# Second layer, both ends: the wait ahead of ScalarE's first square roots is taken off, and the last block's expert steps are placed at other pairs

## The chip, the cores and the metric

The kernel runs on one core of one Trainium2 chip. The metric is the device time of one execution in microseconds (us); where several executions are compared, it is their median. The core has five engines with a program each: TensorE (PE, with its weight loads shown as PEld), VectorE (DVE), ScalarE (ACT), GpSimd (POOL) and SyncE (SP, which here only starts transfers). They meet at semaphores: one engine increments, another waits for a count.

## What is computed

Two transformer-like layers over 4 sequences of 512 tokens with 128 features. Only the second layer is touched. It is, cut to what matters:

```python
# attention of layer 1, for each sequence: X is (512, 128), q and k are (512, 64)
q, k = X @ Wq.T, X @ Wk.T
Vy = X @ Wy_w.T + Wy_b
e = relu(rho(q[:, None, :] + k[None, :, :]))      # rho: signed square root, eps 1e-8
scores = e @ Wphi                                 # (512, 512)
ex = exp(scores - max(scores))
out = (ex @ Vy + (sum_j ex * e) @ We_w.T + We_b * denom) / (denom + 1e-9)
# feed-forward of layer 1: all 8 experts for every token, weighted by the top-2 shares
z = (x @ w1[e] + b1[e]) * (x @ w2[e] + b2[e])
s = silu(z @ wg[e] + bg[e])
out = out + share[:, e] * (s @ w3[e] + b3[e])
x = x + attention + feed_forward
```

## The kernel before

`second_layer` does the attention's pairwise part and the experts at once. The rows of all four sequences are cut into MB = 32 blocks. A block m holds 32 "pairs", numbered by group gg (0 to 7, `GROUPS`) and column c (0 to 3, `QUADS`); a pair is a 128x512 tile of `feat`, which lies in the tensor that the profile calls arena. There are two halves of `feat`, j = 0 and 1, used in turn. Each block also carries one expert for one sequence.

For every pair of a block the kernel does this:

- a **feature**: relu(k + q), on VectorE (line 1037), ScalarE (line 1176) or GpSimd (lines 1305 and 1311);
- a **root**: ScalarE's square root over two groups, 8 pairs, at once (line 1188, 128x4096);
- a **score**: TensorE multiplies by phi and adds into `psS` (line 1328), 4 multiplies a group, which the trace shows as 8 records since fp32 goes through in two passes;
- after a block's last score the maximum and shift on VectorE (`largest`, lines 1043 and 1045), the exponentials on ScalarE (lines 1197 and 1200) and `split` on VectorE (line 1103), which makes `spread`;
- a **broadcast** on TensorE (line 1341), which lays one row of exponentials over all partitions in one of 3 PSUM banks, and a **product** with accumulation on VectorE (`reduce_pair`, line 1051) that uses it. The broadcast of pair k waits until product k - 3 is done, so TensorE runs at most three pairs ahead.

The order on each engine is written out by hand: inside each engine's `tile`, a table `work` says after which (gg, c) which other step is issued. The expert's steps of a block are: left and right product on TensorE (lines 1377 and 1385), z on VectorE (line 1077), `gate` on TensorE (line 1392, four multiplies named (f, half)), tanh on ScalarE (line 1225, which uses the halved gate bias `bgh`), `lift` (add one) on GpSimd (line 1287), `silu` on VectorE (line 1083), `down` on TensorE (line 1405, two halves of four multiplies), and `add_experts` on VectorE (line 1094, four steps of 128x128). The `down` and `add_experts` steps of block m stand in block m + 1.

At the **start** of the layer there is nothing yet to reduce. VectorE makes the features of two whole blocks (a loop of n = 0 to 15 with four features each). After n = 7 it copies the transposed shares (line 1143), halves the shares (line 1145) and halves the gate bias (line 1146, semaphore `bg_halved`). After n = 9 it runs `largest(0, 0)`, and after n = 10 it adds the b3 products (line 1153). ScalarE makes a root for each odd n: the first four belong to block 0. TensorE does scores 0 to 5 of block 0, then 16 small multiplies for b3 (line 1453), then scores 6 and 7.

At the **end**, after block 31's last product, GpSimd copies the accumulated sums (`place`, line 1279, two copies), TensorE runs `combine` (lines 1359 and 1363), and VectorE finishes (lines 1064 to 1069), adds the last expert's output (line 1094), and the result leaves by DMA. In this kernel block 31's `down` stands on TensorE after the last broadcast and ahead of `combine`.

ScalarE's program for the start, the only place in which `bg_halved` is waited for:

```python
act.wait_ge(bg_halved, 1)
for n in range(2 * GROUPS):
    if n % 2:
        roots(n // GROUPS, n // GROUPS, n % GROUPS, ahead=True)
    if n == GROUPS + AHEAD_EXP[1]:
        exponentials(0, 0, before=0)
        keep_left(0, 0, first=True)
```

Of the kernel before, what the change touches and what calls it, by code (L numbers as in the profile page):

```python
# [922 lines left out]
def second_layer(nc, g, sb):  # L923
# [24 lines left out]
    with ExitStack() as ctx:  # L948
# [81 lines left out]
        with nc.Block() as block:  # L1030
            @block.vector
            def _(dve):
# [73 lines left out]
                def tile(t, first=False, last=False):  # L1106
                    for j in range(2):
# [8 lines left out]
                            (4, 0): lambda: none or add_experts(m - 1, 0, first),  # L1116
                            (4, 1): lambda: final or largest(m + 1, 1 - j),
                            (5, 0): lambda: none or add_experts(m - 1, 1),
                            (5, 2): lambda: none or add_experts(m - 1, 2),
                            (5, 3): lambda: none or add_experts(m - 1, 3),  # L1120
                            SILU_AT[0]: lambda: silu(m, 0),
                            SILU_AT[1]: lambda: silu(m, 1),
                            SPLIT_AT: lambda: final or split(m + 1, 1 - j, before=1 if none else 2),
# [44 lines left out]
            def _(act):  # L1168
# [49 lines left out]
                def tanh_half(m, first=False):  # L1218

                    if not first:  # L1220
                        act.wait_ge(y_done, m)
                    for f in range(GT):
                        act.wait_ge(gate_done, m * GT + f + 1)
                        act.sem_inc(act_passed, 1)
                        act.activation(s[:, f, :], (psZ, psX)[f], ACT.Tanh, bias=bgh[:, f, bass.ds(m % E, 1)],
                                       scale=0.5).then_inc(tanh_ready, 1)
# [22 lines left out]

                act.wait_ge(bg_halved, 1)  # L1250
                for n in range(2 * GROUPS):
# [70 lines left out]
            def _(pe):  # L1322
# [87 lines left out]
                def tile(t, first=False, last=False):  # L1410
                    for j in range(2):
# [9 lines left out]
                            (3, 3): lambda: gate(m, 0, 0),  # L1421
                            (4, 1): lambda: gate(m, 0, 1),
                            (4, 3): lambda: gate(m, 1, 0),
                            (5, 1): lambda: gate(m, 1, 1),
                            (6, 1): lambda: transpose_ex(m, j, none),
                            (6, 3): lambda: final or left_product(m + 1, 0, first=1 if none else 0),
                            (0, 2): lambda: none or right_product(m, 0),
# [37 lines left out]
                tile(NT - 1, last=True)  # L1465
                down(MB - 1, 0, last=True)
                down(MB - 1, 1)
                combine(MB - 1, 1, 0)
# [82 lines left out]
```

## Time and profile before

| | |
|---|---|
| median of 3 runs | 1397.66 us (1397.62 to 1400.98) |
| the profiled execution | 1398.52 us |
| its span, first to last instruction | 1396.8 us |
| mean granted TensorE clock | 0.976 of full speed |
| busy: PE, DVE, ACT, POOL | 87%, 87%, 81%, 64% |
| second layer begins | at about 379.5 us |

The profile is of one execution. Its own time is 1.72 us more than its span, and 0.86 us more than the median. A "busy" share is an average over the span, and what binds the kernel has to be read from one stretch at a time. The clock column of the views is the share of full speed that TensorE was granted: 1.00 is 2.4 GHz, 0.50 is 1.2 GHz.

### The profile page before, as it was taken

To read this page: it belongs to the slowest core of one execution; us is meant where nothing else is said; L and a number is where in the kernel's file an instruction comes from. 1 tells how busy PE (TensorE), PEld (TensorE's weight loads), DVE (VectorE), ACT (ScalarE), POOL (GpSimd) and SP (SyncE) were. 2 spreads that over 40 slices of the span, in tenths; PEclk is the share of its full clock that TensorE was granted. 3 is DMA by queue.
4 is the path that set the end of the run, shared out by engine and by line. 5 is a ranking of instruction groups with operands and counts; after the bars stand their busy time and mean duration, and the time that the engine had idled before them with its cause. 6 is when DMAs were issued, how large, how long until landed. Compare 5 with 4: busy or idle time off the path is not lost.

```text
span 1396.8 us, 21175 instructions
## 1 busy us (share of the span) xinstructions
PE 1212.3 (87%) x6185; PEld 579.2 (41%) x6185; DVE 1212.8 (87%) x3409; ACT 1135.3 (81%) x1292; POOL 892.1 (64%) x1294
## 2 busy tenths in 40 slices
PE   3899999997737989998989998989998889998887
PEld 2577767675512333333333333333333333333333
DVE  5777888887658999999998999998999999999997
ACT  1776888885258999989999989999999999998950
POOL 0754733332004888888888878888888888888820
PEclk9999999999668999999999999999999999999999
DMA  6001100000000000010000010000000000001001
GB/s 191 9 11 26 28 1 0 0 1 1 19 0 16 20 19 19 20 31 27 20 20 20 20 31 20 27 20 20 20 23 27 27 20 19 19 20 31 27 20 34
DMA packets 38843, 32.36 MB, mean 23 GB/s; under 512 B 6150, under 2 KB 35609, under 8 KB 38738
## 3 DMA queue, kind: packets, MB, share of 16 engines
q1 hardware_dynamic: 37714, 29.76, 7.3%
q0 software_dynamic: 1024, 1.35, 0.6%
q8 instruction: 47, 0.77, 0.2%
q14 instruction: 58, 0.48, 0.1%
HBM read 29.10 MB, written 2.75 MB: 23 GB/s over the span
## 4 chain that ended last, share of the span: by engine, by line
DVE 36%; PE 31%; issue 5%; ACT 1%; DVEq 0%; ACTq 0%
DVE arena L1051 22%; PE ps L1328 10%; PE ps L1341 9%; DVE arena L1037 6%; PE ps L1405 4%; PE ps L1385 4%; DVE s L1083 3%; DVE x L1094 2%; PE ps L1377 2%; PE ps L1359 2%; DVE spread L1103 2%; DVE nmax L1043 1%; ACT arena L1188 1%; PE ps L1363 0%; DVE shift L1045 0%
## 5 line engine op out<-in xcount | busy, mean ns | idle before, releaser
L1051 DVE SCALAR_TENSOR_TENSOR arena<-arena,ps 128x512 f32<-128x512 f32 x1024 | 663.7, 677 | 68.7 <-PE ps L1341 67.6
L1188 ACT ACTIVATE arena<-arena,eps 128x4096 f32<-128x4096 f32 x128 | 474.1, 3707 | 6.0 <-ACT arena L1176 5.7
L1305 POOL TENSOR_SCALAR arena<-kT,negq 128x512 f32<-128x512 f32 x480 | 345.1, 725 | 179.2 <-DVE arena L1051 170.0
L1341 PE MATMUL ps<-spread,sel 128*128 128x512 f16 x1024 | 357.3, 386 | 100.5 <-DVE arena L1051 94.4
L1311 POOL TENSOR_SCALAR arena<-arena,q 128x512 f32<-128x512 f32 x480 | 349.4, 739 | 22.4
L1341 PEld LDWEIGHTS ps<-spread,sel 128*128 128x128 f16 x1024 | 91.8, 97 | 492.2 <-DVE arena L1051 377.5
L1328 PE MATMUL ps<-arena,phi_cols 128*32 128x512 f32 x2048 | 274.5, 610 | 20.6 <-ACT arena L1188 20.6
L1176 ACT ACTIVATE arena<-kT,q 128x512 f32<-128x512 f32 x330 | 216.9, 712 | 45.2 <-DVE arena L1051 45.2
L462 POOL TENSOR_SCALAR kT<-kT,region 128x512 f32<-128x512 f32 x128 | 89.3, 698 | 155.2 <-DVE region L587 154.6
L512 ACT ACTIVATE kT<-ps,region 128x512 f32<-128x512 f32 x128 | 88.1, 688 | 59.3 <-DVE region L582 57.8
L1392 PE MATMUL ps<-z,wge 128*128 128x512 f32 x256 | 130.8, 592 | 0.3 <-DVE z L1077 0.3
L1037 DVE TENSOR_SCALAR arena<-kT,q 128x512 f32<-128x512 f32 x214 | 119.4, 580 | 0.3 <-PEq L789 0.3
L582 DVE TENSOR_REDUCE region<-ps 128x1 f32<-128x512 f32 x128 | 88.1, 689 | 24.9 <-PE ps L687 23.9
L592 DVE TENSOR_TENSOR pT_lo<-ps,pT_hi 128x512 fp32r<-128x512 f32 x128 | 86.9, 679 | 11.3 <-ACT pT_hi L525 10.9
L1328 PEld LDWEIGHTS ps<-arena,phi_cols 128*32 128x32 f32 x2048 | 40.9, 108 | 127.9 <-issue 103.3
L702 PE MATMUL ps<-ident,kT 128*128 128x128 f32 x512 | 77.4, 274 | 9.3 <-DVE pT_lo L592 9.3
L1051 DVE DVE_READ_ACCUMULATOR arena<-arena,ps 128x1 f32 x1024 | 80.4, 79 | 0.0
L702 PEld LDWEIGHTS ps<-ident,kT 128*128 128x128 f32 x512 | 61.3, 140 | 44.9 <-issue 20.1
L525 ACT ACTIVATE pT_hi<-ps 128x512 fp32r<-128x512 f32 x128 | 75.7, 591 | 2.9 <-PE ps L702 2.2
L1377 PE MATMUL ps<-xnT,w1e 128*128 128x512 f32 x128 | 68.2, 615 | 4.9 <-DVE x L1153 4.9
L1405 PE MATMUL ps<-w3e,s 128*128 128x128 f32 x512 | 68.9, 279 | 2.1 <-DVE s L1083 2.1
L1405 PEld LDWEIGHTS ps<-w3e,s 128*128 128x128 f32 x512 | 69.1, 197 | 4.0 <-DVE s L1083 2.4
(196 smaller groups left out, 1720.8 us busy)
## 6 DMA issues: line engine op xcount, KB each, us to landing
wge<-in_e_wg SPq DMA_DIRECT2D x32, 256.0 KB, 2.7
w1e<-in_e_w SPq DMA_DIRECT2D x32, 128.0 KB, 2.1
w2e<-in_e_w SPq DMA_DIRECT2D x32, 128.0 KB, 2.1
w3e<-in_e_w SPq DMA_DIRECT2D x32, 128.0 KB, 2.2
region<-in_w SPq DMA_DIRECT2D x1, 2048.0 KB
out<-x SPq DMA_DIRECT2D x4, 256.0 KB, 2.9
region<-in_wqk SPq DMA_DIRECT2D x1, 512.0 KB, 4.7
region<-in_wv SPq DMA_DIRECT2D x1, 512.0 KB, 5.4
```

The lines of the kernel that those rows point to most:

```text
L702: ins = pe.transpose(ps[:, TBK[late % 2], m * P:(m + 1) * P], ex[:, late % 4, m * P:(m + 1) * P], g.ident[:])
L1037: dve.tensor_scalar(feat[:, j, QUADS * gg + c, :], kT[:, bass.ds(b * N, N)], q2[:, bass.ds(pair0 + GROUPS * c + gg, 1)], 0.0, ALU.add, ALU ...
L1051: dve.scalar_tensor_tensor(feat[:, j, k, :], feat[:, j, k, :], 1.0, psB[:, k % BANKS, :], ALU.mult, ALU.mult, accum_out=sums[:, j, gg, c:c ...
L1176: act.activation(feat[:, j, QUADS * gg + c, :], kT[:, bass.ds(b * N, N)], ACT.Relu, bias=q2[:, bass.ds(pair0 + GROUPS * c + gg, 1)]).then_ ...
L1188: act.activation(grp, grp, ACT.Sqrt, bias=eps[:]).then_inc(e_ready, 2)
L1305: pool.tensor_scalar(feat[:, j, QUADS * gg + c, :], kT[:, b * N:(b + 1) * N], HUGE, negq[:, b % 2, at - b * N // 2:at - b * N // 2 + 1], A ...
L1311: pool.tensor_scalar(f, f, 1.0, q2[:, at:at + 1], ALU.mult, ALU.add).then_inc(pool_feat, 1)
L1328: ins = pe.matmul(psS[32 * c:32 * (c + 1), :], phi_cols[:, gg, :], feat[:, j, QUADS * gg + c, :], start=(gg == 0), stop=(gg == GROUPS - 1))
L1341: pe.matmul(psB[:, k % BANKS, :], sel[:, gg, c, :], spread[:, j, :], start=True, stop=True).then_inc(bc_done, 1)
L1377: pe.matmul(psY, w1[:, f * P:(f + 1) * P], xnT[:, bass.ds(m // E * N, N)], start=True, stop=True).then_inc(left_done, 1)
L1392: ins = pe.matmul((psZ, psX)[f], wg[:, half * DFF + f * P:half * DFF + (f + 1) * P], z[:, half, :], start=(half == 0), stop=(half == 1))
L1405: ins = pe.matmul(psY[:, i * D:(i + 1) * D], s[:, f, i * P:(i + 1) * P], w3[:, f * D:(f + 1) * D], start=(f == 0), stop=(f == GT - 1))
```

## The change

Three things change. ScalarE's wait for `bg_halved` moves from ahead of the first root to ahead of the first tanh (block 0). In the last block (`final`, m = 31) the gate multiplies stand after pairs (3,3), (4,0), (4,1) and (4,2) where they stood after (3,3), (4,1), (4,3) and (5,1); VectorE's `silu` steps after (5,1) and (6,0) where they stood after (7,0) and (7,2); and its `add_experts` steps 1 to 3 (of block 30) after (4,1), (4,2) and (4,3) where they stood after (5,0), (5,2) and (5,3). And block 31's two halves of `down` stand after broadcasts (7,1) and (7,2), where they stood after the last broadcast. No instruction is added or removed.

```diff
@@ VectorE, tile: the table work
-                            (4, 1): lambda: final or largest(m + 1, 1 - j),
-                            (5, 0): lambda: none or add_experts(m - 1, 1),
-                            (5, 2): lambda: none or add_experts(m - 1, 2),
-                            (5, 3): lambda: none or add_experts(m - 1, 3),
-                            SILU_AT[0]: lambda: silu(m, 0),
-                            SILU_AT[1]: lambda: silu(m, 1),
+                            **({} if final else {(4, 1): lambda: largest(m + 1, 1 - j)}),
+                            **({(4, 1): lambda: add_experts(m - 1, 1), (4, 2): lambda: add_experts(m - 1, 2),
+                                (4, 3): lambda: add_experts(m - 1, 3)} if final else
+                               {(5, 0): lambda: none or add_experts(m - 1, 1),
+                                (5, 2): lambda: none or add_experts(m - 1, 2),
+                                (5, 3): lambda: none or add_experts(m - 1, 3)}),
+                            **({(5, 1): lambda: silu(m, 0), (6, 0): lambda: silu(m, 1)} if final else
+                               {SILU_AT[0]: lambda: silu(m, 0), SILU_AT[1]: lambda: silu(m, 1)}),
@@ ScalarE, tanh_half
                     if not first:
                         act.wait_ge(y_done, m)
+                    else:
+                        act.wait_ge(bg_halved, 1)
@@ ScalarE, the start
-                act.wait_ge(bg_halved, 1)
                 for n in range(2 * GROUPS):
@@ TensorE, tile: the table work
-                            (4, 1): lambda: gate(m, 0, 1),
-                            (4, 3): lambda: gate(m, 1, 0),
-                            (5, 1): lambda: gate(m, 1, 1),
+                            (4, 1) if not final else (4, 0): lambda: gate(m, 0, 1),
+                            (4, 3) if not final else (4, 1): lambda: gate(m, 1, 0),
+                            (5, 1) if not final else (4, 2): lambda: gate(m, 1, 1),
                             (6, 1): lambda: transpose_ex(m, j, none),
+                            **({(7, 1): lambda: down(m, 0, last=True), (7, 2): lambda: down(m, 1)} if final else {}),
@@ TensorE, after the last tile
                 tile(NT - 1, last=True)
-                down(MB - 1, 0, last=True)
-                down(MB - 1, 1)
                 combine(MB - 1, 1, 0)
```

How the instructions stand on the engines, at three places. A row is a line of the kernel, an operation, what it writes and reads, and how many stand in a row; line numbers of the changed kernel are 2 to 4 higher.

ScalarE at the start of the second layer, with the semaphores that each row waits for. Before:

```order
L1188 ACT_TABLE_LOAD [waits feat_ready,bg_halved]
L1188 ACTIVATE arena<-arena,eps 128x4096
L1188 ACTIVATE arena<-arena,eps 128x4096 [waits feat_ready] x3
L1197 ACT_TABLE_LOAD
L1197 ACTIVATE ex<-ps,shift 128x512 [waits shift_ready]
```

And now:

```order
L1190 ACT_TABLE_LOAD [waits feat_ready]
L1190 ACTIVATE arena<-arena,eps 128x4096
L1190 ACTIVATE arena<-arena,eps 128x4096 [waits feat_ready] x3
L1199 ACT_TABLE_LOAD
L1199 ACTIVATE ex<-ps,shift 128x512 [waits shift_ready]
```

The order is the same; the first table load has one semaphore less to wait for, and the load itself stands behind the remaining wait.

TensorE in block 31, from the second gate multiply (`gate(31, 0, 1)`) on. Before:

```order
L1392 MATMUL ps<-z,wge 128x512
L1341 MATMUL ps<-spread,sel 128x512 x2
L1392 MATMUL ps<-z,wge 128x512
L1341 MATMUL ps<-spread,sel 128x512 x2
L1392 MATMUL ps<-z,wge 128x512
L1341 MATMUL ps<-spread,sel 128x512 x4
L1349 MATMUL ps<-ident,ex 128x128 x4
L1341 MATMUL ps<-spread,sel 128x512 x6
L1405 MATMUL ps<-w3e,s 128x128 x8
L1359 MATMUL ps<-V,exT 128x129 x4
```

And now, down to the last broadcast:

```order
L1395 MATMUL ps<-z,wge 128x512
L1344 MATMUL ps<-spread,sel 128x512
L1395 MATMUL ps<-z,wge 128x512
L1344 MATMUL ps<-spread,sel 128x512
L1395 MATMUL ps<-z,wge 128x512
L1344 MATMUL ps<-spread,sel 128x512 x7
L1352 MATMUL ps<-ident,ex 128x128 x4
L1344 MATMUL ps<-spread,sel 128x512 x4
L1408 MATMUL ps<-w3e,s 128x128 x4
L1344 MATMUL ps<-spread,sel 128x512
L1408 MATMUL ps<-w3e,s 128x128 x4
L1344 MATMUL ps<-spread,sel 128x512
```

Between two gate multiplies there is one broadcast where there were two, and the two halves of `down` stand ahead of the last two broadcasts.

VectorE in block 31, from pair (4,1) on. Before:

```order
L1051 SCALAR_TENSOR_TENSOR arena,sums<-arena,ps 128x512 x4
L1094 SCALAR_TENSOR_TENSOR x<-ps,share,x 128x128
L1051 SCALAR_TENSOR_TENSOR arena,sums<-arena,ps 128x512 x2
L1094 SCALAR_TENSOR_TENSOR x<-ps,share,x 128x128
L1051 SCALAR_TENSOR_TENSOR arena,sums<-arena,ps 128x512
L1094 SCALAR_TENSOR_TENSOR x<-ps,share,x 128x128
L1051 SCALAR_TENSOR_TENSOR arena,sums<-arena,ps 128x512 x5
L1083 SCALAR_TENSOR_TENSOR s<-ps,bge,s 128x512
L1051 SCALAR_TENSOR_TENSOR arena,sums<-arena,ps 128x512 x2
L1083 SCALAR_TENSOR_TENSOR s<-ps,bge,s 128x512
L1051 SCALAR_TENSOR_TENSOR arena,sums<-arena,ps 128x512
```

And now:

```order
L1051 SCALAR_TENSOR_TENSOR arena,sums<-arena,ps 128x512
L1094 SCALAR_TENSOR_TENSOR x<-ps,share,x 128x128
L1051 SCALAR_TENSOR_TENSOR arena,sums<-arena,ps 128x512
L1094 SCALAR_TENSOR_TENSOR x<-ps,share,x 128x128
L1051 SCALAR_TENSOR_TENSOR arena,sums<-arena,ps 128x512
L1094 SCALAR_TENSOR_TENSOR x<-ps,share,x 128x128
L1051 SCALAR_TENSOR_TENSOR arena,sums<-arena,ps 128x512 x2
L1083 SCALAR_TENSOR_TENSOR s<-ps,bge,s 128x512
L1051 SCALAR_TENSOR_TENSOR arena,sums<-arena,ps 128x512 x3
L1083 SCALAR_TENSOR_TENSOR s<-ps,bge,s 128x512
L1051 SCALAR_TENSOR_TENSOR arena,sums<-arena,ps 128x512 x7
```

The three `add_experts` steps (line 1094) and the two `silu` steps (line 1083) come earlier; seven products instead of one follow the second `silu`.

## Rows read from the trace of the kernel before

**Rows 1.** The page: PE's and DVE's busy time, and engines of the last-ending chain.

```profile
PE 1212.3 (87%) x6185; PEld 579.2 (41%) x6185; DVE 1212.8 (87%) x3409; ACT 1135.3 (81%) x1292; POOL 892.1 (64%) x1294
...
DVE 36%; PE 31%; issue 5%; ACT 1%; DVEq 0%; ACTq 0%
```

**Rows 2.** Instructions in order of time, layer's start: start, us, engine, line, idle before.

```profile
379.53 13.07 DVE L1037 TENSOR_SCALAR arena<-kT,q 128x512 f32<-128x512 f32 x32 [0.32 <-PEq L789]
...
395.05 0.15 DVE L1146 TENSOR_SCALAR bgh<-bge 128x16 f32<-128x16 f32 x1
395.13 3.24 DVE L1037 TENSOR_SCALAR arena<-kT,q 128x512 f32<-128x512 f32 x8
395.28 1.28 ACT L1188 ACT_TABLE_LOAD   x1 [17.05 <-DVE bgh L1146]
396.58 14.51 ACT L1188 ACTIVATE arena<-arena,eps 128x4096 f32<-128x4096 f32 x4
...
415.79 0.69 DVE L1043 TENSOR_REDUCE nmax<-ps 128x1 f32<-128x512 f32 x1 [17.41 <-PE ps L1328]
...
428.47 0.74 DVE L1103 SCALAR_TENSOR_TENSOR spread<-exh,split_by,ex 128x512 f16<-128x512 f16 x1
```

**Rows 3.** The chain of waits between 407 and 416: start, us, what.

```profile
407.54 1.92 PE ps L1328 x16
409.46 3.76 PE ps L1453 x32
413.22 2.54 PE ps L1328 x16
```

**Rows 4.** Windows: stretch, its us, busy (and count) by engine, clock, DMA.

```profile
383.80:403.90 20.10, 3.56 (x16) 0.59 (x16) 14.57 (x37) 8.61 (x4) 0.00 (x0) 0.50 0.00 1
404.10:414.50 10.40, 8.75 (x76) 4.73 (x76) 0.00 (x0) 8.27 (x3) 0.00 (x0) 0.99 0.00 0
...
428.10:434.60 6.50, 5.33 (x13) 1.60 (x17) 4.79 (x14) 6.50 (x3) 3.09 (x5) 0.50 0.01 3
...
450.00:480.00 30.00, 27.24 (x144) 10.40 (x143) 27.96 (x82) 28.30 (x26) 24.88 (x37) 1.00 0.09 23
1383.70:1387.00 3.30, 0.98 (x3) 0.19 (x2) 3.30 (x10) 0.00 (x0) 0.00 (x0) 1.00 0.00 0
1387.10:1390.40 3.30, 3.13 (x14) 3.13 (x15) 0.72 (x3) 0.00 (x0) 0.47 (x2) 0.50 0.00 0
1390.50:1392.00 1.50, 1.46 (x13) 1.27 (x12) 0.00 (x0) 0.00 (x0) 0.00 (x0) 1.00 0.00 0
```

**Rows 5.** Instructions in order of time, last block: down of block 30, gates, products.

```profile
1370.72 1.05 PE L1405 MATMUL ps<-w3e,s 128*128 128x128 f32 x8
...
1375.41 1.02 PE L1392 MATMUL ps<-z,wge 128*128 128x512 f32 x2
...
1376.26 0.35 DVE L1094 SCALAR_TENSOR_TENSOR x<-ps,share,x 128x128 f32<-128x128 f32 x1
1376.27 0.59 PE L1341 MATMUL ps<-spread,sel 128*128 128x512 f16 x2
...
1376.52 0.68 DVE L1051 SCALAR_TENSOR_TENSOR arena<-arena,ps 128x512 f32<-128x512 f32 x1
...
1377.12 0.68 DVE L1051 SCALAR_TENSOR_TENSOR arena<-arena,ps 128x512 f32<-128x512 f32 x1
```

**Rows 6.** The same view, behind the last product.

```profile
1387.13 0.68 DVE L1051 SCALAR_TENSOR_TENSOR arena<-arena,ps 128x512 f32<-128x512 f32 x1
...
1387.27 3.58 PE L1405 MATMUL ps<-w3e,s 128*128 128x128 f32 x16 [2.15 <-DVE s L1083]
...
1387.88 0.53 POOL L1279 COPY sumsT<-sums 64x32 f32<-64x32 f32 x2 [7.25 <-DVE arena L1051]
...
1390.68 1.06 PE L1359 MATMUL ps<-V,exT 128*128 128x129 f32 x8
...
1392.00 0.16 DVE L1064 TENSOR_SCALAR den<-ps 128x1 f32<-128x1 f32 x1 [4.18 <-PE ps L1363]
```

## The prediction

> **What bounds the kernel now.** The page comes first. PE and DVE are both busy for 87% of the span, and the chain that ended last is made of them: DVE 36%, PE 31%, ACT 1% [rows 1]. An average like that says that the middle of the kernel is bound by these two in turn, and that a change to ScalarE's waiting can only matter where ScalarE is alone on the path. So the view to read is not the page but the order of time at the two places that the diff touches.
>
> At the start of the second layer, VectorE makes 32 features in 13.07 us, copies the shares and ends with the halved bias at 395.05 + 0.15. ScalarE's first table load stands at 395.28, after 17.05 us without work, and the trace names the halved bias as what released it. The roots follow at once: four of them from 396.58 for 14.51 us. VectorE then has 8 more features until 398.4 and stands still for 17.41 us, until the maximum of block 0 can be taken at 415.79 [rows 2]. The chain between the two is scores 4 and 5 (released by the third root), the b3 products, and scores 6 and 7: 1.92 + 3.76 + 2.54 us on PE [rows 3]. Here ScalarE, and then PE, do set the end, with every other engine waiting.
>
> In the last block VectorE goes from product to product every 0.60 us (1376.52 to 1377.12) [rows 5]. After the last one (end 1387.81) comes a stretch in which VectorE waits 4.18 us, until 1392.00. PE's `down`, begun at 1387.27, holds `combine` back until 1390.68, though GpSimd's copies that combine also needs are done at 1387.88 + 0.53 = 1388.41 [rows 6].
>
> **The first roots.** Without the bias, the first root needs the first 8 features. 32 take 13.07 us, so one takes 0.408 and 8 take 3.27: they are there at 379.53 + 3.27 = 382.80. From the bias (ready 395.20) to the first root (396.58) it took 1.38 us, table load included [rows 2]; the load stands behind the remaining wait, so I charge it in full: first root at about 384.15 instead of 396.58, 12.4 us earlier. Does it keep that lead? Each root takes 14.51 / 4 = 3.63 us, the 8 features for the next one 3.27, so ScalarE never catches up with VectorE. Features made beside a running root took 3.24 / 8 = 0.405 us each against 0.408 alone [rows 2], so I charge nothing for the two engines at work together.
>
> What is late next? The first half of block 0's scores now falls beside VectorE's features. The b3 products need VectorE's copies; these are done about 395.0, and PE comes to them at 409.46 - 12.4 = 397.0, 2 us later, so they don't stop it. PE's last score then ends at about 403.4. VectorE is there at 398.4 and still waits 5.0 us. The wait shrinks from 17.4 to 5.0 and doesn't vanish: the whole 12.4 us come off the path, and VectorE's own work would have let through 17.4. Behind this point the exponentials, the b3 adds, 24 features and `split` (428.47) are in the same order and all start relative to the maximum; from there every step of every block waits for semaphores of the steps before it, the weight loads too, so a lead is handed on. The weights of expert 0 are asked for at the layer's start, far ahead of either time.
>
> The wait itself moves ahead of the first tanh, where behind it are queued block 0's tanh and ScalarE's roots and features of block 2. The bias is ready at 395.2 in both kernels, and the first tanh comes behind 20 products of block 0, which start behind `split` (428.47, and by the sum 416.1 then) [rows 2]: nothing.
>
> **What the clock does to this.** It was 0.50 from 383.8 to 403.9, 0.99 until 414.5 although PE was busy for 8.75 of those 10.4 us, and 0.50 again in 428.1 to 434.6, where PE had 5.33 us of work [rows 4]. The b3 products (3.76 us) ran in the high stretch; at half the clock they would take up to 3.76 more, and the last scores (2.54, the end of it behind 414.5, already at 0.50) up to 1 more. On the other side, the 5.3 us of PE work after 428.1 would take 2.7 less at full clock. So the opening is worth 12.4, between 12.4 - 4.8 = 7.6 and 12.4 + 2.7 = 15.1. I take 12.4 because PE's work has the same order and the same gaps as before, only earlier, and keep both ends for the range, since one trace can't show whether the clock's changes move along with the work. The Trainium skill ("TensorE: Matmul & The Clock Gate", Part 1) says that the clock's monitor runs freely and doesn't restart with the kernel, so that its changes need not move along with the work. No row here shows that or speaks against it; by that rule the sum could come out anywhere between the two ends.
>
> **The last block.** Three gates now come one broadcast apart. A gate holds PE for 1376.27 - 1375.41 = 0.86 us, a broadcast for about 0.22 (two take 0.59 with the second's way out), together 1.08. A product with an `add_experts` step takes VectorE 0.60 + 0.26 = 0.86 [rows 5]. So PE loses 0.2 us a pair over three pairs, 0.65 in all, against a lead of at most three pairs that the first gate has already eaten: I lay the steps out and get a stall of 0.3 (0.1 at the second product, 0.2 at the third); bounds 0 and 0.8. `tanh` and `lift` come to `silu` in time: the fourth gate ends near 1378.3, each of the two handles one 128x512 tile as a product does (0.68), and VectorE reaches the second silu's place only near 1382. The silu and add steps themselves only change places among VectorE's work: nothing.
>
> The two halves of `down` now stand ahead of the last two broadcasts. At full clock a half takes 1.05 us (block 30's) [rows 5]. Count from the end of product 26, when broadcast 29 may go: PE does broadcast 29, half a `down` and broadcast 30 by 0.35 + 1.05 + 0.3 = 1.7, and VectorE wants it after products 27 to 29 at 1.8: in time. The second half and broadcast 31 come at about 3.0, and VectorE wants it at 2.4: a stall of 0.55. At half clock a half takes 3.58 / 2 = 1.79 [rows 6], and the same count gives a stall of about 2.3.
>
> What it buys: `combine` no longer stands behind `down`. After the last product GpSimd's copies end 0.60 later, PE needs 0.1 to see it and 1.3 for combine (1390.68 to 1392.00): VectorE goes on 2.05 us after its last product instead of 4.19. That is 2.15 gained, less 0.3 and 0.55: **1.3 us** at full clock. With combine at half clock about 1.1 less, so 0.2; with `down` there too, 1.75 less again, a loss of 1.5. The clock stood at 1.00 in 1383.7 to 1387.0 with PE busy for only 0.98 of 3.3 us, and fell as `down` began (0.50 from 1387.1 to 1390.4) [rows 4]. In the changed kernel PE works at just that place and then has a gap of 1.4 us ahead of combine. I take 0.7, between the first two values.
>
> **The sum.** 12.4 + 0.7 = 13.1 us. Against the profiled execution's own 1398.52 this is 1385.4; that execution was 0.86 above the median, so on the median's scale 1397.66 - 13.1 = about **1384.5 us**.
>
> **The rivals.**
> - *The clock takes part of the opening.* The clock's changes don't move with the work and the b3 products fall into a stretch at half clock: 3.7 us of the 12.4 go, 1388.2 us. For: it fell during the b3 products' end in the old trace though PE was busy. Against: the same work in the same order had the high clock before. 14%.
> - *The end loses.* `down` runs at half clock ahead of the last broadcasts and VectorE stands for 2.3 us: -1.5 in place of +0.7, 1386.7 us. For: the light use just ahead of it. Against: the clock was still high there before. 14%.
> - *The opening gains more,* since the work after `split` meets a high clock: 12.4 + 2.7 + 0.7, 1381.8 us or a little less. 7%.
> - *No change, since the wait wasn't what held.* If the lead were absorbed later by something that doesn't move (a transfer, GpSimd), the time would stay at 1397 give or take 4. Against it: VectorE's 17.41 us are idle time with a semaphore from PE at its end, and nothing behind it waits for a fixed time. 3%.
> - *Slower.* In a block at full clock, PE is busy for 27.24 of 30 us [rows 4]. If PE did not get its high clock back through the first block of products, which it now meets at another moment, that block would take up to 27.2 us longer for PE, some 24 after the slack: 1384.5 + 24 = 1408.5 us. It decides from about 16 us of block work at half clock on (13.1 of 24, times 30). Against: in the old trace the clock came back after 6.5 us at this place, with the same work. 2%.
> - The forecast itself, 1382.5 to 1387: 60%.
>
> **How the numbers follow.** The first two rivals pull up, the third down. From 1381.5 to 1388.5 lie the forecast, the end's loss, most of the clock's case and most of the better opening, about 85 in 100. A measurement of this kernel can tell about 0.3% (4.2 us) from no change. The forecast, the first three rivals are all faster by more than that: 95 in 100; same 3, slower 2; I move one point to "same" for mixtures.
>
> **What would show it.** In the new trace: the first root near 384.2, not 396.6; `largest` of block 0 near 403.4 with about 5 us of wait; `split` near 416.0. In the steady blocks nothing. In block 31 a wait of VectorE for a broadcast of some 0.3 us in group 4 and of some 0.55 at the last pair, and about 2.05 us, not 4.19, between the last product and line 1064's step. The forecast is wrong if `largest` waits much over 5 us (then b3 or the clock is the cause), if the first root waits for something not named here, or if the distance from `split` to the last product, 959 us, changes by more than 3 us.

## The result, and the profile after

| | before | after |
|---|---|---|
| median | 1397.66 us (3 runs, 1397.62 to 1400.98) | 1383.25 us (3 runs, 1383.03 to 1383.37) |
| profiled execution | 1398.52 us, span 1396.8 | 1383.03 us, span 1381.3 |
| ratio | | 0.9889, 95% interval 0.9866 to 0.9911 |

The change made the kernel 14.4 us faster by the medians, and 15.5 by the two spans. The forecast was 1384.5. The page answers to [rows 1] and says little, as before:

```profile
PE 1210.2 (88%) x6185; PEld 575.5 (42%) x6185; DVE 1212.5 (88%) x3409; ACT 1135.1 (82%) x1292; POOL 888.8 (64%) x1294
```

Busy time has hardly moved (PE 2.1 us, DVE 0.3 us less); what shrank is waiting. In order of time, the start of the second layer of the kernel after, which answers to [rows 2]:

```profile
379.38 1.28 ACT L1190 ACT_TABLE_LOAD   x1 [4.96 <-DVE arena L1037]
380.68 14.51 ACT L1190 ACTIVATE arena<-arena,eps 128x4096 f32<-128x4096 f32 x4
...
391.64 1.92 PE L1331 MATMUL ps<-arena,phi_cols 128*32 128x512 f32 x16 [0.87 <-ACT arena L1190]
...
397.86 3.64 PE L1331 MATMUL ps<-arena,phi_cols 128*32 128x512 f32 x16
...
401.57 0.69 DVE L1043 TENSOR_REDUCE nmax<-ps 128x1 f32<-128x512 f32 x1 [7.00 <-PE ps L1331]
```

ScalarE's wait is 4.96 us in place of 17.05 and is now for features. VectorE's wait for the maximum is 7.00 in place of 17.41. But line 1043 has moved by 415.79 - 401.57 = 14.2 us, which is more than the 12.1 us of waiting that ScalarE lost. Of the 14.2 us, 3.8 stand ahead of the layer, in code that no edit touches. In these traces an fp32 multiply leaves two records, an fp16 broadcast or a transpose one; that the two records are two passes, no row shows beyond their count. So the 16 router multiplies of line 901 have 32 records. Here they are in the kernel before, and then after, in the view of one line (shortest, median and longest in ns, first and last start):

```profile
L901 PE MATMUL psL<-region,xnT x32: 222/361/361, 359.1 to 365.5; 128*128 128x8 f32 x32
```

```profile
L901 PE MATMUL psL<-region,xnT x32: 223/256/361, 358.6 to 362.2; 128*128 128x8 f32 x32
```

The same multiplies took 3.0 us less (3.83 for 6.83), out of 3.8 us by which the layer began sooner. Their stretch in the windows view (the clock is the third number from the right), before and then after:

```profile
359.00:365.90 6.90, 6.90 (x35) 6.90 (x34) 0.82 (x6) 0.60 (x1) 0.00 (x0) 0.50 0.00 0
```

```profile
358.60:362.50 3.90, 3.90 (x34) 3.90 (x34) 0.79 (x7) 0.60 (x1) 0.00 (x0) 0.94 0.00 0
```

So I cut both traces at the same instructions. Each number is the distance between two starts in the view by time (the next section has the same table for the experiments):

| stretch | before | after | less |
|---|---|---|---|
| program's start to the layer's first feature | 379.53 | 375.73 | 3.80 |
| first feature to the maximum of block 0 | 36.26 | 25.84 | 10.42 |
| maximum to split | 12.68 | 12.68 | 0 |
| split to product 8 of block 31, that of pair (2,0) | 941.27 | 941.45 | -0.18 |
| product 8 to the last product | 17.39 | 18.05 | -0.66 |
| last product to line 1064's step | 4.87 | 2.76 | 2.11 |
| from there to the end | 4.80 | 4.79 | 0.01 |

Of the 15.5 us, then, 10.4 are the opening, 1.45 the last block (2.11 - 0.66), and 3.8 lie ahead of every edit. The two edited stretches together gave 11.9.

The last block of the kernel after, in order of time, answers to [rows 5, 6]:

```profile
1371.34 1.05 PE L1408 MATMUL ps<-w3e,s 128*128 128x128 f32 x8
...
1372.44 1.05 PE L1408 MATMUL ps<-w3e,s 128*128 128x128 f32 x8
...
1373.75 0.69 DVE L1051 SCALAR_TENSOR_TENSOR arena<-arena,ps 128x512 f32<-128x512 f32 x1 [0.27 <-PE ps L1344]
...
1374.51 0.53 POOL L1282 COPY sumsT<-sums 64x32 f32<-64x32 f32 x2 [8.73 <-DVE arena L1051]
...
1375.09 1.16 PE L1362 MATMUL ps<-V,exT 128*128 128x129 f32 x8 [1.38 <-POOL sumsT L1282]
...
1376.51 0.16 DVE L1064 TENSOR_SCALAR den<-ps 128x1 f32<-128x1 f32 x1 [2.07 <-PE ps L1366]
```

`combine` now waits for GpSimd's copies and not for `down`; VectorE waits 2.07 us in place of 4.18 ahead of line 1064, and pays 0.27 ahead of the last product.

### The profile page after: what moved, and what is told of

Same layout as the page of the kernel before. It is cut to its first block, busy times and chain, and to the rows that moved or that the text cites. A ratio compares the mean times of both kernels' runs of the same rounds, so it can differ in the third digit from the quotient of the medians.

```text
span 1381.3 us, 21175 instructions
## 1 busy us (share of the span) xinstructions
PE 1210.2 (88%) x6185; PEld 575.5 (42%) x6185; DVE 1212.5 (88%) x3409; ACT 1135.1 (82%) x1292; POOL 888.8 (64%) x1294
## 4 chain that ended last, share of the span: by engine, by line
DVE 35%; PE 32%; issue 5%; ACT 1%; POOL 0%; POOLq 0%; DVEq 0%; ACTq 0%
DVE arena L1051 21%; PE ps L1331 10%; PE ps L1344 9%; DVE arena L1037 5%; PE ps L1388 4%; PE ps L1408 4%; DVE s L1083 3%; DVE x L1094 2%; PE ps L1380 2%; PE ps L1362 2%; DVE spread L1103 2%; DVE nmax L1043 1%; PE ps L1366 1%; ACT arena L1190 1%; DVE shift L1045 0%
## 5 line engine op out<-in xcount | busy, mean ns | idle before, releaser
L1314 POOL TENSOR_SCALAR arena<-arena,q 128x512 f32<-128x512 f32 x480 | 348.0, 735 | 22.4
L1388 PE MATMUL ps<-xnT,w2e 128*128 128x512 f32 x128 | 67.3, 608 | 0.3 <-DVE z L1077 0.3
```

Of the source, the lines that this page charges most:

```text
L1314: pool.tensor_scalar(f, f, 1.0, q2[:, at:at + 1], ALU.mult, ALU.add).then_inc(pool_feat, 1)
L1388: pe.matmul(psX, w2[:, f * P:(f + 1) * P], xnT[:, bass.ds(m // E * N, N)], start=True, stop=True).then_inc(right_done, 1)
```

## The experiments

Twelve kernels went to the chip in three groups, each group beside its own runs of the kernel before (medians 1396.81, 1397.67 and 1397.65 us). Single executions of the kernel before lay between 1392.69 and 1401.18. That spread is as large as some of the effects asked about, so the verdicts on stretches rest on the traces, one for each kernel, cut at the same instructions. Each expectation names the theory under test as Theory A and what else it could be as the rival. In the table all numbers are us; the third and the fourth column count from the layer's first feature:

| kernel | layer's first feature at | to first root | to maximum | product 8 to last | last to line 1064 |
|---|---|---|---|---|---|
| before | 379.53 | 17.05 | 36.26 | 17.39 | 4.87 |
| c0_copy | 379.25 | 17.05 | 36.29 | 17.39 | 4.81 |
| after | 375.73 | 4.95 | 25.84 | 18.05 | 2.76 |
| a0_after | 379.39 | 4.95 | 25.17 | 20.05 | 2.76 |
| e1_open | 379.59 | 4.95 | 25.17 | 17.38 | 5.95 |
| e2_ends | 379.80 | 17.04 | 35.61 | 20.05 | 2.76 |
| e3_mid | 374.28 | 8.19 | 28.14 | 17.39 | 6.02 |
| e4_b3_last | 374.11 | 4.95 | 21.50 | 20.06 | 2.76 |
| e5_b3_first | 374.11 | 4.95 | 22.40 | 20.03 | 2.76 |
| e6_spread | 375.81 | 4.94 | 25.95 | 17.83 | 2.76 |
| e7_b3_spread | 379.45 | 4.94 | 21.50 | 17.39 | 3.08 |
| e8_fill_end | 377.23 | 4.95 | 21.50 | 17.44 | 2.76 |
| e9_b3_oldend | 377.38 | 4.95 | 21.50 | 17.39 | 6.07 |
| e10_fill_route | 379.82 | 4.94 | 21.50 | 17.39 | 3.00 |

(a0_after and after are one kernel, c0_copy and before another.)

The second column has a pattern of its own. The first layer has router multiplies of the same form (line 336), which no edit touches either. They too come in two durations, here in the kernel before and in e4_b3_last:

```profile
17.24 6.84 PE L336 MATMUL psL<-gw,xnT 128*128 128x8 f32 x32
```

```profile
16.98 3.81 PE L336 MATMUL psL<-gw,xnT 128*128 128x8 f32 x32
```

Where both lines take 6.8 us, the second layer begins at 379.25 to 379.82. Where line 901 alone is shorter (3.83 in after, 3.72 in e6_spread), it begins at 375.73 and 375.81; where line 336 alone is (4.46 in e8_fill_end, 4.03 in e9_b3_oldend), at 377.23 and 377.38; where both are (e3_mid, e4_b3_last, e5_b3_first), at 374.11 to 374.28. So the whole spread of 5.7 us in the layer's start goes with these two lines.

**c0_copy**: the kernel before, no edit.

> The kernel before, unedited, timed against itself. In the two traces the second layer began 3.8 us earlier in the changed kernel (375.73 against 379.53), 3.0 us of it in the 32 router multiplies of line 901 (3.83 against 6.83 us), which no edit touches. Theory A (clock by chance): within 1 us of the kernel before in time, but the trace may show line 901 at either duration, and single executions differ by up to 3.5 us. Rival B (a property of each program): line 901 again takes 6.8 us and the executions agree within 0.3 us.

Measured: 1397.76 us median (1392.76 to 1399.23), ratio 0.9997 (0.9982 to 1.0012). Line 901 took 6.83 us again in this trace, but in other kernels with the same code up to there it took 6.84 (e7_b3_spread, e9_b3_oldend), 4.42 (e4_b3_last) and 3.72 (e6_spread), and the changed kernel itself showed both: 3.83, and 6.83 in a0_after. Rival B falls: it is no property of the program. The executions differ by 6.5 us, more than the 3.5 expected; the median is within the 1 us expected.

**e1_open**: the opening's edit alone.

```diff
-                act.wait_ge(bg_halved, 1)            # ahead of the first root
...
+                        act.wait_ge(bg_halved, 1)    # ahead of the first tanh
```

> The kernel before with only the wait for the halved bias moved from ahead of the first root to ahead of the first tanh. Theory A: the first root starts 4.95 us after the layer's first feature (17.05 before), the maximum of block 0 comes 25.8 us after it (36.3 before): 10.4 us faster where TensorE's clock is low for the last scores, up to 12.1 where it is high. Rival B (the opening alone made all of the difference): 14.4 us faster. Rival C (the ends carried a good part, the opening under 8).

Measured: 1387.47 us (1385.77 to 1388.04), ratio 0.9933 (0.9911 to 0.9955), that is 9.4 us faster (6.3 to 12.4). First root after 4.95 us, maximum after 25.17: 11.1 us less in this trace. Theory A holds. 14.4 lies outside the interval, and "under 8" is against the trace, though not outside the interval.

**e2_ends**: the last block's edits alone.

```diff
@@ against the kernel after: the wait goes back
-                    else:
-                        act.wait_ge(bg_halved, 1)
...
+                act.wait_ge(bg_halved, 1)
                 for n in range(2 * GROUPS):
```

> The changed kernel with ScalarE's wait put back ahead of the first root, so that only the last block's order differs from the kernel before. Theory A: from the last product to line 1064's step 2.1 us less (2.76 against 4.87 from start to start), 0.7 us more inside block 31: 1.4 us faster, about 1396.2. Rival: down's multiplies run at half clock ahead of the last broadcasts, and it is 1.5 us slower.

Measured: 1397.01 us (1393.8 to 1398.47), ratio 0.9999 (0.9987 to 1.0010): no difference. The trace says why. The rows of `down` and the last two products, in order of time:

```profile
1384.19 1.91 PE L1407 MATMUL ps<-w3e,s 128*128 128x128 f32 x8
...
1386.33 1.85 PE L1407 MATMUL ps<-w3e,s 128*128 128x128 f32 x8
1386.57 0.69 DVE L1051 SCALAR_TENSOR_TENSOR arena<-arena,ps 128x512 f32<-128x512 f32 x1 [1.01 <-PE ps L1343]
1388.01 0.38 PE L1343 MATMUL ps<-spread,sel 128*128 128x512 f16 x1
1388.43 0.69 DVE L1051 SCALAR_TENSOR_TENSOR arena<-arena,ps 128x512 f32<-128x512 f32 x1 [1.16 <-PE ps L1343]
```

and that stretch in the windows view:

```profile
1381.60:1387.80 6.20, 5.63 (x21) 4.02 (x20) 4.66 (x15) 0.38 (x1) 0.00 (x0) 0.50 0.00 0
```

The clock was at 0.50 from 1381.6 to 1387.8, half a `down` took 1.9 us in place of 1.05, and VectorE waited 1.01 and 1.16 us for the last two broadcasts. From product 8 to the last one it is 20.05 us in place of 17.39; the 2.1 won behind the last product don't cover this. The rival's mechanism is what this trace shows; its price was 1.5 us, and it came to 20.05 + 2.76 - 17.39 - 4.87 = 0.55.

**e3_mid**: the wait stays, the bias is ready earlier.

```diff
+                    if n == 3:
+                        dve.tensor_scalar(bgh[:], bg[:], 0.5, None, ALU.mult).then_inc(bg_halved, 1)
                     if n == GROUPS - 1:
...
-                        dve.tensor_scalar(bgh[:], bg[:], 0.5, None, ALU.mult).then_inc(bg_halved, 1)
```

> The kernel before with ScalarE's wait where it was, and VectorE's halving of the bias made after 16 features in place of 32 features and the copies. Theory A (the gain is the time at which the first root starts, until something else is late): bias ready 6.7 us after the layer's first feature, first root at 8.2 us, 8.9 us earlier than before, 3.2 us later than in the changed kernel; 7 to 9 us faster than before. Rival (something else but this wait held the opening): no change, or the whole 12.

Measured: 1389.38 us (1385.87 to 1391.29), ratio 0.9949 (0.9932 to 0.9966), 7.1 us faster (4.8 to 9.5).

```profile
381.17 1.28 ACT L1189 ACT_TABLE_LOAD   x1 [8.20 <-DVE bgh L1141]
382.47 14.51 ACT L1189 ACTIVATE arena<-arena,eps 128x4096 f32<-128x4096 f32 x4
```

The first root came at 8.19 us (8.2 expected). Taking off 8.9 us of the wait brings the maximum 8.1 us sooner, nearly in step with the first root (scores 6 and 7 took 3.32 us here and 2.58 before, which is most of the difference): 17.05, 8.19 and 4.95 us to the root, 36.3, 28.1 and 25.2 to 25.8 to the maximum. Theory A holds; neither "no change" nor "the whole 12" does.

**a0_after**: the kernel after, again.

> The changed kernel, unedited, on the same chip as the next three. Segments from traces of the earlier runs: opening (first feature to the maximum of block 0) 10.4 to 11.1 us shorter, block 31 to line 1064's step between 1.4 us shorter and 0.6 us longer by where the clock falls. Theory A: 1396.8 - 11.2 = about 1385.5 median, single executions 1382 to 1389. Rival (the first 14.4 us were the edit's own): 1382.5.

Measured: 1384.8 us (1379.32 to 1386.68), ratio 0.9897 (0.9863 to 0.9931). The median is near Theory A's 1385.5, and 2.3 us off the rival's 1382.5; one of the four executions, 1379.32, lies below the 1382 to 1389 expected. In this trace the layer began at 379.39, the opening took 25.17 and the last block 20.05, just as in e2_ends. So the same kernel that gained 1.45 us at its end in the first trace lost 0.55 in this one.

**e4_b3_last**: b3 behind the last score.

```diff
                 for gg in range(GROUPS):
-                    if gg == GROUPS - 2:
-                        for t in range(NT): ...      # the 16 b3 multiplies
                     scores(0, 0, gg, first=True)
+                for t in range(NT): ...              # the same multiplies
```

> The changed kernel with TensorE's b3 multiplies behind the last score of block 0 instead of ahead of scores 6 and 7. Theory A (behind the first roots TensorE is what the opening waits for, and the b3 multiplies stand in its way without need): the maximum comes about 4 us sooner, 21.5 us after the first feature in place of 25.8, and the b3 multiplies then run beside the maximum and four features, VectorE waiting 1 to 2 us for them: split 2 to 4 us sooner, 2 to 4 us faster than the changed kernel. Rival (ScalarE's fourth root sets it, at 19.5 us, and TensorE catches up): under 1 us.

Measured: 1376.97 us (1375.67 to 1380.49), ratio 0.9857 (0.9824 to 0.9889). The maximum comes after 21.50 us in place of 25.2 to 25.8, in this kernel and in the four others that have this order and edit.

```profile
393.62 1.92 PE L1331 MATMUL ps<-arena,phi_cols 128*32 128x512 f32 x16 [1.68 <-ACT arena L1190]
395.47 2.05 PE L1456 MATMUL ps<-b,z 8*128 8x128 f32 x16
395.61 0.69 DVE L1043 TENSOR_REDUCE nmax<-ps 128x1 f32<-128x512 f32 x1 [2.66 <-PE ps L1331]
```

TensorE now waits for the fourth root (1.68 us), scores 6 and 7 follow it at once, and VectorE waits 2.66 us where it waited 7.00. The 1 to 2 us of wait for b3 that I had expected do not appear: the adds follow the four features directly. This shows that b3, not ScalarE, was the last to be late in the kernel after. By the median it is 7.8 us under a0_after; between the two traces the order gives 3.7 us (4.3 against the first trace of the kernel after), and 5.3 lie ahead of the layer (374.11 against 379.39).

**e5_b3_first**: the copies early, b3 ahead of score 0.

```diff
-                    if n == GROUPS - 1:
+                    if n == 1:
                         dve.wait_ge(shareT_done, 1)
...
-                    if gg == GROUPS - 2:
+                    if gg == 0:
```

> The changed kernel with VectorE's copies of the shares after the first 8 features in place of 32, and TensorE's b3 multiplies ahead of score 0, where TensorE only waits for the first root. Theory A: the second root waits up to 0.5 us for its features, the maximum comes at about 21.7 us after the first feature in place of 25.8: 4 us faster than the changed kernel. Rival (the copies push the roots back by their own 2.4 us): 2 us or less.

Measured: 1381.06 us (1376.62 to 1383.97), ratio 0.9886 (0.9848 to 0.9924). Maximum after 22.40 us, 0.7 more than expected: the second root waited 0.78 us for its features. Theory A holds in mechanism, with 2.8 to 3.4 us in place of 4; it is 0.9 us worse than e4's order. By the medians it is 3.7 us under a0_after, with the layer beginning 5.3 us sooner in its trace, so the medians do not price the order.

**e6_spread**: more room between TensorE's steps in block 31.

```diff
-                            (4, 1) if not final else (4, 0): lambda: gate(m, 0, 1),
-                            (4, 3) if not final else (4, 1): lambda: gate(m, 1, 0),
-                            (5, 1) if not final else (4, 2): lambda: gate(m, 1, 1),
+                            (4, 1): lambda: gate(m, 0, 1),
+                            (4, 3): lambda: gate(m, 1, 0),
+                            (5, 1): lambda: gate(m, 1, 1),
...
-                            **({(7, 1): lambda: down(m, 0, last=True), (7, 2): lambda: down(m, 1)} if final else {}),
+                            **({(6, 3): lambda: down(m, 0, last=True), (7, 1): lambda: down(m, 1)} if final else {}),
...
-                            **({(5, 1): lambda: silu(m, 0), (6, 0): lambda: silu(m, 1)} if final else
+                            **({(5, 1): lambda: silu(m, 0), (6, 1): lambda: silu(m, 1)} if final else
```

> The changed kernel with the last block's gates at the places of the kernel before, the second silu one pair later, and the two halves of down after pairs (6,3) and (7,1), two broadcasts apart. Theory A (the closeness of these multiplies on TensorE is what stalls VectorE): no wait at pairs (4,2), (4,3) and 31, so 0.65 us less from pair (2,0) to the last product where the clock is high, and where it is low about 1 us of stall in place of 2.7. Rival (the stalls are of something else): as the changed kernel.

Measured: 1382.74 us (1378.9 to 1384.25), ratio 0.9888 (0.9856 to 0.9920). From product 8 to the last one 17.83 us: one wait was left, since `down` now waited 0.88 us for the second silu. That is 0.22 us less than in the kernel after, where 0.65 was expected. The clock stayed high through this block, so what the theory says of the low clock was not tested. The next run sets that silu one pair earlier.

**e7_b3_spread**: e4's order at the start, the spread last block with silu after (5,1) and (6,0).

> The changed kernel with both gains put together: TensorE's b3 multiplies behind the last score, and in the last block the gates at their old places, silu after (5,1) and (6,0), and down after (6,3) and (7,1). Theory A: maximum at 21.5 us after the first feature as with the b3 move alone; block 31 from pair (2,0) to the last product 17.4 to 17.6 us, with no wait of VectorE for a broadcast where the clock is high, and under 19 where it is low: about 1376.5 median, 8 us under the changed kernel and 20 under the kernel before. Rival: the last block gives nothing back, and it is as the b3 move alone (1377).

Measured: 1380.05 us (1378.58 to 1381.5), ratio 0.9877 (0.9857 to 0.9897). Both stretches came as expected (21.50; 17.39 with no stall, at the high clock; a low one did not occur here either), yet the median is 3.5 us above the 1376.5 that I had written. In this trace the layer began at 379.45, 5.3 us later than in e4's, from which I had taken the level. I had made the very mistake that c0_copy warns of. Set against the kernel before on the same chip it is 17.6 us faster.

**e8_fill_end**: e7 and multiplies that only keep TensorE busy.

```diff
                                 broadcast(m, j, gg, c, warm=not none)
+                                if final and gg >= 4 and (gg, c) not in work and (gg, c) < (7, 2):
+                                    pe.matmul(psS, sel[:, gg, c, :], spread[:, j, :], start=True, stop=True)
```

> The same, with one more multiply (128x512, result not used) on TensorE after each pair of block 31's groups 4 to 7 that has no other TensorE step: it only keeps TensorE at work. Theory A (the last block varies because the clock falls while TensorE has little to do): the clock stays high to the end in the trace and block 31 to the last product takes 17.4 to 17.8 us every time; median 1 us under the run without it. Rival (the clock falls for another reason, or the added multiplies delay the broadcasts): block 31 is longer, 18 to 21 us.

Measured: 1379.68 us (1378.19 to 1381.44), ratio 0.9881 (0.9861 to 0.9901). The clock, in two windows of block 31 and what follows it:

```profile
1353.00:1368.00 15.00, 13.79 (x68) 7.40 (x67) 15.00 (x47) 1.76 (x3) 1.24 (x2) 1.00 0.22 62
1368.00:1372.00 4.00, 1.83 (x13) 1.19 (x10) 1.90 (x8) 0.00 (x0) 0.46 (x2) 1.00 0.00 0
```

It stays at 1.00 from 1353.0 to 1372.0, through `combine`. The same stretch of e7_b3_spread, without filler, up to its last product:

```profile
1353.00:1371.30 18.30, 15.28 (x69) 7.75 (x68) 18.30 (x58) 1.76 (x3) 1.24 (x2) 1.00 0.17 51
```

So the clock was high there without filler too. The two stretches take 20.20 us together, against 20.47 in e7. That is the shortest end of all, but by so little that one trace can't tell it from chance, and the medians don't separate the two. The run shows that the filler does no harm, not that it is needed once the steps stand apart.

**e9_b3_oldend**: e4's start with the last block of the kernel before.

> The kernel before with the wait moved off the first root and the b3 multiplies behind the last score, and its own last block. Beside the other runs it prices the last block alone. From the traces so far, pair (2,0) to line 1064's step takes 22.2 to 23.4 us with this end, 20.8 to 22.8 with the changed one. Theory A (the end is worth 0.5 to 1.5 us, by where the clock falls): 2 us slower than the first run of this group, 0.5 to 1 slower than the b3 move alone. Rival (the ends are worth nothing): equal to both.

Measured: 1383.1 us (1379.04 to 1384.93), ratio 0.9897 (0.9877 to 0.9916), 3.05 us above e7. Its last product to line 1064 took 6.07 us and its wait there was 5.4:

```profile
DVE den L1064 <- PE ps L1364: 5.4, 1, 5.4
```

So the spread last block is worth 23.46 - 20.47 = 3.0 us beside the old one in these two traces. It is not always that much: the trace of the kernel before has 22.26, which makes it 1.8. The medians differ by about the same 3.05, but this is weak support, for the executions of the two kernels overlap and the intervals of the ratios do as well. I had expected 2. Against the b3 move alone (e4_b3_last, another chip) the last block of the trace is 0.6 us longer (23.46 against 22.82), inside the 0.5 to 1 expected; the medians are 6.1 apart, and 3.3 us of that kind lie ahead of the layer in the traces.

**e10_fill_route**: e7 and five filler multiplies ahead of the router's transposes.

```diff
+            for _ in range(5):
+                pe.matmul(psP[:, 1, :], g.ident[:], g.xnT[:, 0:512], start=True, stop=True)
```

> The first kernel of this group with five more multiplies (128x512, result not used) on TensorE at the beginning of the stretch that normalizes and routes, ahead of the transposes, where TensorE waits 9.5 us for VectorE. It tests where the time ahead of the second layer goes. Theory A (it is TensorE's clock): line 901's 32 multiplies take 3.8 us in place of up to 6.8 and the second layer begins 31 us or less after that stretch starts, in place of 31.1 to 35.1: 1 to 4 us faster. Rival (chance of another kind): 31 to 35 us as before.

Measured: 1381.11 us (1378.58 to 1381.63), ratio 0.9881 (0.9861 to 0.9901). Line 901's role took 6.84 us again, and the layer began 35.2 us after the stretch started: the forecast failed.

```profile
345.04 4.56 PE L893 MATMUL psP<-xnT,ident 128*128 128x512 f32 x10
354.55 4.32 PE L896 MATMUL psX<-ident,region 128*128 128x128 f32 x16 [4.96 <-DVE region L848]
358.66 6.84 PE L903 MATMUL psL<-region,xnT 128*128 128x8 f32 x32
```

The filler still met the high clock, so it was done in 4.56 us, at 349.6, and TensorE then stood for 4.96 us. The clock was still at 1.00 until 353.5, where the kernel before has 0.50 from 350.0 on, but had fallen when the transposes began; these took 4.32 us as in the kernel before. It doesn't speak against the clock as the cause (the clock did fall in between), but it is no proof either: filler that ends 5 us before the work it should help has tested nothing. Filler that reaches up to the transposes wasn't tried.

## Why the prediction was right, point by point

The time (1383.25 for 1384.5) was right, and the sum of 13.1 us lies between what the two groups that timed the unedited pair gave (14.4 and 12.9). The first of these was helped by chance, and so is the closeness of the forecast: in that trace the two edited stretches gave 11.9 us (10.4 + 1.45) where 13.1 was forecast, and 3.8 came from ahead of the layer; in a0_after they gave 10.5 (11.1 - 0.55).

- **First root.** Forecast 4.62 us after the first feature, measured 4.95: 12.1 us in place of 12.4. The wait for features ended 0.3 us later than eight times 0.408 gave.
- **ScalarE keeps its lead, nothing else waits for the features.** Right: four roots in 14.51 us as before, and VectorE's 32 features took 13.07 us with the roots beside them, as they had without.
- **What is late next.** Named rightly, TensorE with b3 and the last scores; its size was forecast by the old trace's clock. b3 took 4.36 us of the chain in place of 3.76, and scores 6 and 7 took 3.62 in place of 2.54:

```profile
391.64 1.92 PE ps L1331 x16
393.56 4.36 PE ps L1457 x32
397.93 3.62 PE ps L1331 x16
```

  The clock was at 0.50 from 396.6 on. That is the first rival's mechanism, at 1.7 us in place of 3.7; in a0_after and e1_open it took 1.0. The prediction's own sign for it came: `largest` waited 7.00 us where 5 was forecast. Its ground for charging nothing, that the same work in the same order would meet the same clock, does not hold: the clock fell 17.7 us after the first root in the kernel before, 15.9 in the kernel after, 16.4 in a0_after and 21.8 in e2_ends, whose opening is that of the kernel before. With 0.3 for the root this turns 12.4 into 10.4, and 11.1 in the other two traces. Here the prediction did not ask the next question: b3 isn't needed for the maximum at all, and e4_b3_last shows 3.7 to 4.3 us waiting there.
- **From the maximum on, everything just moves.** Right: 12.68 us to split in all fourteen traces, give or take 0.01. The distance from split to the last product changed by 0.84 us, within the 3 that were allowed. The steady blocks moved by between -1.3 and +0.9 from trace to trace on their own.
- **The last block.** Stalls of 0.3 and 0.55 us were forecast, 0.66 in all came out (0.27 at the last pair). The gain behind the last product was forecast at 2.15, measured 2.11. At the high clock this makes 1.45 (forecast 1.3). But the case that I had at 14%, `down` at half clock, is in four of the five traces with this last block (18.05 us in the kernel after, but 20.05, 20.05, 20.06 and 20.03 in a0_after, e2_ends, e4_b3_last and e5_b3_first). The chance was far too low. A loss of 1.5 was forecast for it, 0.55 came, since `combine` then met the high clock. On the other side the old end isn't fixed at 4.87 either: 5.95, 6.02 and 6.07 in e1_open, e3_mid and e9_b3_oldend. Average against average, 22.9 us for the five old ends and 22.4 for the five new ones, the last block's edit is worth about half a microsecond, and e2_ends alone can't be told from nothing. The four traces with the steps further apart (e6_spread, e7_b3_spread, e8_fill_end, e10_fill_route) took 20.2 to 20.6, each with the clock at 1.00 up to the last product. Whether the spacing keeps the clock up, or chance did, no run shows.
- **What was missed.** No step of the prediction had the 3.8 us ahead of the layer. Line 901 took from 3.72 to 6.84 us in these traces with no edit near it (five filler multiplies in e10_fill_route aside), line 336 the same range, and the layer's first feature came between 374.11 and 379.82.

What stays open: why the clock is up in one execution at lines 336 and 901 and not in another, where the program is the same. The rows show only that it is so.

## What to carry to other kernels

Where an engine waits for a product that it needs only much later, look for what was meant to be covered by that wait: moving one wait of ScalarE from its first instruction to the first one that needs the value took 10.4 to 11.1 us off the opening, and the trace's "idle before, released by" on that one row had the whole story. After taking such a wait away, ask what stands in the way of the next event on the engine that is now late; here 16 multiplies that nobody waited for yet were worth another 3.7 to 4.3 us. And before giving a difference of a few microseconds to an edit, cut both traces at the same instructions and look at the stretches that were not edited.

## What the runs showed of the hardware

- Executions of one unchanged program, on several chips, spread by 8.5 us (1392.69 to 1401.18), and by 7.7 on one chip (1392.76 to 1400.47), which I hadn't expected after three runs of which two lay within 0.04 us. Where it is visible in the traces it is TensorE's clock: lines 336 and 901 (each 3.7 to 6.8 us), the last scores of block 0, `down` and `combine`. The Trainium skill ("TensorE: Matmul & The Clock Gate", Part 1) says that the monitor behind the clock runs freely and is not reset by a kernel's start; the same multiplies at both levels in the same program agree with that.
- A multiply that is moved out of an idle end into a lightly used stretch can meet the low clock there and hold up work that was free of it before: half a `down` took 1.05 or 1.9 us at the same place in the program (after, e2_ends).
- The multiplies of b3 (8 rows, 128 columns) kept TensorE busy without a gap, and yet the clock fell to 0.50 at or just behind them in both the kernel before (about 414.3, mid-way through scores 6 and 7) and the kernel after (about 396.6, in the last b3 multiplies); in e2_ends it fell only at 418.6, behind the last score. In the first two a busy share of 1.0 in the windows was followed by a fall; why, no run shows.
